# An attention stage on one core: one query tile with all sixteen heads as the unit, scores in four row tiles, and the weighting of values half a batch later

## The reference, cut to what matters

```python
q = proj(query, Wq, bq); k = proj(key, Wk, bk); v = proj(value, Wv, bv)   # query: LayerNorm of the rows
scores = einsum('bhqd,bhkd->bhqk', q, k) * 0.25 + mask * -1e9
attn = softmax(scores, axis=-1)
ctx = einsum('bhqk,bhkd->bhqd', attn, v)        # then back to (b, s, 256)
x = x + ctx @ Wo.T + bo
```

## Time and profile before

| what | value |
|---|---|
| median of 3 runs | 937.86 us |
| the profiled execution, its own time | 935.81 us, of which the span is 934.0 us |
| PE, DVE, ACT, POOL busy over the span | 690.8, 714.8, 386.6, 133.5 us |
| mean granted TensorE clock | 0.888 |
| attention, from the first statistics to the last aggregation | 357.8 to 650.6 us |

### The profile page before, as it was taken

The page is one execution under the profiler, slowest core; times in us unless marked ns, Lnnn a source line. Parts: engine busy times, 40 slices in busy tenths (PEclk is TensorE's granted clock), DMA queues, the critical chain, the costliest instruction groups (busy, mean ns, idle before and its releaser), DMA issues.

```text
span 934.0 us, 13856 instructions
## 1 busy us (share of the span) xinstructions
PE 690.8 (74%) x3693; PEld 477.1 (51%) x3694; DVE 714.8 (77%) x1743; ACT 386.6 (41%) x646; POOL 133.5 (14%) x165
## 2 busy tenths in 40 slices
PE   4599853989988885899999999994033666665674
PEld 2487642656566653577776777773021333343343
DVE  4388885565555556888888888887988899999995
ACT  1343311232232320443433434333145787777773
POOL 4547651212212121000000000000000000000000
PEclk9799986999999995999999999998557788778887
DMA  9586533111121118000000000000000000000001
GB/s 326 159 322 227 186 117 95 47 47 47 52 62 53 42 44 314 3 0 0 0 0 0 0 0 0 0 0 2 1 0 1 1 22 23 11 11 22 22 23 45
DMA packets 31362, 54.33 MB, mean 58 GB/s; under 512 B 4877, under 2 KB 24222, under 8 KB 30176
## 3 DMA queue, kind: packets, MB, share of 16 engines
q1 hardware_dynamic: 25184, 39.81, 12.8%
q0 software_dynamic: 5568, 13.58, 4.2%
q10 hardware_dynamic: 576, 0.55, 0.2%
HBM read 39.90 MB, written 15.89 MB: 60 GB/s over the span
## 4 chain that ended last, share of the span: by engine, by line
DVE 32%; PE 25%; issue 17%; ACT 8%; DMA 7%; SPq 4%; POOL 3%; DVEq 2%; POOLq 1%; ACTq 0%
PE bank L1060 6%; PE bank L1033 3%; PE quad L1019 3%; PE quad L1007 3%; DMA x_after_ffn<-row,niU 2%; DVE hh L1903 2%; DMA row<-rows_by_expert 2%; SPq L408 2%; DVE ctxs L1854 2%; PE bank L1223 2%; POOL x_after_ffn L506 2%; DMA xg<-in_x,idxu 2%; PE bank L1048 2%; SPq L409 1%; DVE ctxs L1842 1%
## 5 line engine op out<-in xcount | busy, mean ns | idle before, releaser
L1223 PE MATMUL bank<-dT,hqT 128*128 128x256 bf16 x256 | 53.3, 379 | 44.7 <-ACT hqT L780 44.7
L953 PE MATMUL bank<-W2s,hidT 128*128 x320 | 76.0, 386 | 12.2 <-ACT hidT L619 12.2
L615 ACT ACTIVATE hid<-hid 128x512 f32<-128x512 f32 x40 | 25.2, 631 | 125.1 <-DVE hid L1517 125.1
L1060 PEld LDWEIGHTS bank<-nVB,nPT 128*128 128x128 f32 x512 | 63.3, 191 | 23.9 <-ACT nPT L677 23.1
L953 PEld LDWEIGHTS bank<-W2s,hidT 128*128 128x128 f32 x320 | 59.3, 190 | 28.3 <-issue 21.7
L936 PE MATMUL quad<-W1s,xts 128*128 x160 | 73.0, 600 | 0.0
L1019 PE MATMUL quad<-nKB,nQT 128*128 128x512 f32 x132 | 71.6, 626 | 1.0 <-ACT nQT L655 0.9
L1060 PE MATMUL bank<-nVB,nPT 128*128 128x34 f32 x512 | 65.5, 273 | 0.0
L506 POOL DMA_INDIRECT x_after_ffn<-row,niU x40 | 39.3, 983 | 168.4 <-DVE row L1526 156.5
L1223 PEld LDWEIGHTS bank<-dT,hqT 128*128 128x128 bf16 x256 | 31.8, 132 | 57.3 <-ACT hqT L780 47.4
L673 ACT ACTIVATE nS<-nS 128x512 f32<-128x512 f32 x64 | 40.8, 637 | 38.3 <-DVE nS L1665 37.0
(11 more groups left out here) (322 smaller groups left out, 1581.7 us busy)
## 6 DMA issues: line engine op xcount, KB each, us to landing
row<-rows_by_expert SPq DMA_DIRECT2D x44, 134.0 KB, 2.1
W1s<-in_ctxO SPq DMA_DIRECT2D x4, 1024.0 KB, 7.9
ctxs<-in_ctxT SPq DMA_DIRECT2D x4, 1024.0 KB, 12.7
W1s<-in_W SPq DMA_DIRECT2D x8, 512.0 KB
W2s<-in_W SPq DMA_DIRECT2D x8, 512.0 KB
X<-x_after_ffn SPq DMA_DIRECT2D x8, 512.0 KB, 7.7
out<-yo SPq DMA_DIRECT2D x16, 256.0 KB, 2.1
b1s<-in_b SPq DMA_DIRECT2D x1, 2048.0 KB
```

The lines of the kernel that those rows point to most:

```text
L953: ins = pe.matmul(bank[6 + u % 2][:, 0:D], hidT[:, u % 2, c, :], W2s[:, bass.ds(ex, 1), c, :].rearrange("p o s -> p (o s)"), start=c == 0, ...
L1060: ins = pe.matmul(bank[7][:, n * 2 * VW:(n + 1) * 2 * VW], nPT[j % 2][:, k, :], nVB[h][:, n, :], start=True, stop=True)
L1223: ins = pe.matmul(bank[(1, 7)[u // 2]][:, (u % 2) * D:(u % 2 + 1) * D], hqT[:, u % 2, c, :], dT[:, c, :], start=c == 0, stop=c == FT - 1)
```

## The change

It touches the narrow branch alone.

- The unit is a query tile with all 16 heads: `nS` is 128x1024, `nM` has 16 maxima, `nPT` is 128x1024.
- `score(b, q)` is 8 matmuls (c = 0, 1 and k = 0 to 3). Each has 32 partitions of `nQT` (two heads) as stationary operand and 128 columns of `nKB`, which is now only 2 heads wide (a new tile `own2` masks it). The four k go to four row tiles of the array and to four PSUM banks.
- Banks 2 to 5 hold both the scores (`scored`, columns 0 to 255 of each) and the transposed probabilities (`turned`, columns 256 to 511). So `score` waits until ScalarE has copied `turned` (n_pTe), and `probs_in` until VectorE has read `scored` (n_add).
- `shift(b, q)` is one add and one reduction of 128x1024 and two subtractions of 128x512. `exps` are two of 128x512, `probs_out` one copy of 128x1024, `probs_in` eight transposes, `weigh` eight matmuls.
- `rows_norm` moves from VectorE to ScalarE, as an activation with the scale rs2 and the bias nm2 = -mean x rs2 (one small instruction in `inverse_rows`).
- The order of the calls changes: `probs_in`, `weigh`, `divide`, `project` and `add_rows` of a query tile stand half a batch later against `score` and `shift`, so the scores of batch b+1 stand in batch b, and a half pass more runs after the loop. Before the loop `shift(0, 0)`, `shift(0, 1)` and `keys_values(1)` stand among `some_stats`. `weight_sizes` stands before the last three `add_rows`.
- Queries go through bank 6 in place of bank 2, and GpSimd copies the context one batch further ahead.

```diff
--- before.py
+++ after.py
...
-        nKB = [sb(f"nKB{h}", [P, DC, HG * KW], F32, en) for h in range(2)]
+        nKB = [sb(f"nKB{h}", [P, DC, 2 * KW], F32, en) for h in range(2)]
+        own2 = sb("own2", [P, 2], F32, en)
...
-        nS = [sb(f"nS{h}", [P, HG, KW], F32, en) for h in range(2)]
-        nM = [sb(f"nM{h}", [P, HG], F32, en) for h in range(2)]
+        nS = [sb(f"nS{h}", [P, NH, KW], F32, en) for h in range(2)]
+        nM = [sb(f"nM{h}", [P, NH], F32, en) for h in range(2)]
...
-        nPT = [sb(f"nPT{h}", [P, HG // 2, P], F32, en) for h in range(2)]
+        nPT = [sb(f"nPT{h}", [P, 4, 2 * P], F32, en) for h in range(2)]
...
+        scored, turned = quad[:, :, 0:2 * P], quad[:, :, 2 * P:4 * P]
...
+                def rows_norm(bt):
+                    act.wait_ge(n_ct, bt)
+                    for q in range(2):
+                        t = bt * 2 + (q + 1)
+                        act.activation(xn3[:, q, :], X2[:, bass.ds(t, 1), :].rearrange("p o d -> p (o d)"), ACT.Identity,
+                                       bias=nm2[:, bass.ds(t, 1)], scale=rs2[:, bass.ds(t, 1)]).then_inc(n_xn, 1)
...
+                def exps(b, q):
+                    for k in range(2):
+                        act.wait_ge(n_sub, b * 4 + (2 * q + k + 1))
+                        half = nS[q][:, HG * k:HG * k + HG, :]
+                        ins = act.activation(half, half, ACT.Exp)
+                    ins.then_inc(n_exp, 1)
+                def probs_out(b, q):
+                    act.wait_ge(n_pT, b * 2 + (q + 1))
+                    act.copy(nPT[q][:], turned).then_inc(n_pTe, 1)
+                def batch(b, h, first=False, last=False, end=False):
+                    if not first:
+                        values_out(b - 1, 0)
+                        probs_out(b - 1, 1)
+                    if not last and not end:
+                        rows_out(b + 1)
+                    if not end:
+                        exps(b, 0)
+                    if not last and not end:
+                        rows_norm(b + 2)
+                        queries_out(b + 1, 1 - h)
+                    if not first:
+                        values_out(b - 1, 1)
+                    if not end:
+                        probs_out(b, 0)
+                        exps(b, 1)
...
+                def score(b, h, q, first=False):
+                    if q == 0:
+                        pe.wait_ge(n_qe, b + 1)
+                        pe.wait_ge(n_kb, b + 1)
+                    if first:
+                        if q:
+                            pe.wait_ge(n_add, 1)
+                    else:
+                        pe.wait_ge(n_pTe, b * 2 + (q - 1))
+                    for c in range(DC):
+                        for k in range(4):
+                            w = slice(32 * k, 32 * k + 32)
+                            ins = pe.matmul(scored[:, k, c * P:(c + 1) * P], nQT[h][w, c, q * P:(q + 1) * P], nKB[h][w, c, :],
+                                            start=True, stop=True)
+                    ins.then_inc(n_S, 1)
+                def probs_in(b, q, last=False):
+                    pe.wait_ge(n_exp, b * 2 + (q + 1))
+                    pe.wait_ge(n_add, b * 2 + (q + 1 if last else q + 2))
+                    for c in range(DC):
+                        for k in range(4):
+                            ins = pe.transpose(turned[:, k, c * P:(c + 1) * P],
+                                               nS[q][:, 4 * k + 2 * c:4 * k + 2 * c + 2, :].rearrange("p h s -> p (h s)"), ident[:])
+                    ins.then_inc(n_pT, 1)
+                def weigh(b, h, q, first=False):
+                    pe.wait_ge(n_pTe, b * 2 + (q + 1))
                     if not first:
...
+                        pe.wait_ge(n_cn, b * 2 + q)
+                    for c in range(DC):
+                        for k in range(4):
+                            n = 4 * c + k
+                            ins = pe.matmul(bank[7][:, n * 2 * VW:(n + 1) * 2 * VW], nPT[q][:, k, c * P:(c + 1) * P], nVB[h][:, n, :],
+                                            start=True, stop=True)
+                    ins.then_inc(n_pv, 1)
...
+                def batch(b, h, first=False, second=False, last=False, end=False):
+                    if not last and not end:
+                        keys_values(b + 1, 1 - h)
+                    if not first:
+                        project_turn(b - 1, 0, first=second)
+                        probs_in(b - 1, 1, last=end)
+                        project(b - 1, 0)
+                    if not last and not end:
+                        rows_in(b + 1)
+                    if not end:
+                        score(b, h, 1, first=first)
+                    if not first:
+                        weigh(b - 1, 1 - h, 1)
+                    if not last and not end:
+                        queries(b + 1)
+                    if not first:
+                        project_turn(b - 1, 1)
+                    if not end:
+                        probs_in(b, 0)
+                    if not first:
+                        project(b - 1, 1)
+                    if not last and not end:
+                        score(b + 1, 1 - h, 0)
+                    if not end:
+                        weigh(b, h, 0, first=first)
...
+                def shift(b, q):
+                    v.wait_ge(n_S, b * 2 + (q + 1))
+                    tt(nS[q][:].rearrange("p (k m) s -> p k m s", k=4), scored.rearrange("p k (m s) -> p k m s", m=4),
+                       maskS[:, q, S - KW:S].unsqueeze(1).unsqueeze(1).broadcast_to([P, 4, 4, KW]), ALU.add).then_inc(n_add, 1)
+                    v.wait_ge(n_add, b * 2 + (q + 1))
+                    red(nM[q][:], nS[q][:], AX.X, ALU.max).then_inc(n_max, 1)
+                    v.wait_ge(n_max, b * 2 + (q + 1))
+                    for k in range(2):
+                        half = nS[q][:, HG * k:HG * k + HG, :]
+                        tt(half, half, bc(nM[q][:, HG * k:HG * k + HG], KW), ALU.subtract).then_inc(n_sub, 1)
...
+                def batch(b, h):
+                    divide(b - 1, 0)
+                    add_rows(b - 1, 0)
+                    new_stats(b - 1, 0)
+                    shift(b, 1)
+                    divide(b - 1, 1)
+                    keys_values(b + 1, 1 - h)
+                    add_rows(b - 1, 1)
+                    new_stats(b - 1, 1)
+                    shift(b + 1, 0)
+                stn.link(red(own2[:], ownh[:].rearrange("p (r t) -> p t r", t=2), AX.X, ALU.add))
+                inverse_rows(0, stn)
+                keys_values(0, 0)
                 some_stats(1, stn)
...
+                some_stats(2, stn)
+                shift(0, 0)
+                some_stats(3, stn)
+                some_stats(4, stn)
+                some_stats(5, stn)
+                shift(0, 1)
+                keys_values(1, 1)
+                for k in range(6, NTILE // 4):
                     some_stats(k, stn)
                 inverse_rows(1, stn)
...
+                shift(1, 0)
+                with v.Fori(0, NB // 2 - 1) as i:
+                    stn.enter(i, 8)
+                    batch(i * 2 + 1, 1)
+                    batch(i * 2 + 2, 0)
+                    stn.leave(NB // 2 - 1)
+                b = NB - 1
+                divide(b - 1, 0)
+                add_rows(b - 1, 0)
+                new_stats(b - 1, 0)
+                shift(b, 1)
+                divide(b - 1, 1)
                 weight_sizes()
...
+                add_rows(b - 1, 1)
+                new_stats(b - 1, 1)
+                for q in range(2):
+                    divide(b, q)
+                    add_rows(b, q)
+                    ins = new_stats(b, q)
+                stn.link(ins)
```

More of the change, by code:

```diff
@@ L1026, in project_turn @@
+                def project_turn(b, q, first=False):
+                    pe.wait_ge(n_cn, b * 2 + (q + 1))
+                    if not first:
+                        pe.wait_ge(n_fin, b * 2 + q)
                     for k in range(DC):
```

222 lines of the change are left out of this document (68 added, 154 removed).

## The result

The changed kernel takes 949.48 us (median of 4 runs, 947.01 to 950.82), the kernel before beside it 937.35: a ratio of 1.013, with an interval of 1.010 to 1.016. It is slower, by 12.1 us where 6.4 were forecast. In the two profiled executions (950.27 and 935.81) all of the difference lies in attention: from the first statistic to the next stage's first reciprocal it takes 358.51 to 669.31 = 310.80 us, before 357.82 to 654.18 = 296.36.

The account below looks back on a forecast made before the run. A chain of waits per half batch bounds the changed loop: terms sum to 8.28 us, taken as 8.17, 29 halves 236.9. With the parts around the loop, attention is +6.4: 935.81 becomes 942.2, median 944 us, range 931 to 963.

Parts of the forecast that it names:

- signs of being wrong: Adds waiting for scores, a batch pace under 15.5 us, or a granted clock in attention below 1 would refute the forecast.
- to the end of the aggregations: Behind the loop, from `weight_sizes` at 640.3 us: reductions, three open query tiles and aggregations, ending at 660.2.
- The chain: Loop: `divide`, `project_turn`, `probs_in`, `project`, `add_rows`, `new_stats` and `shift` wait for one another, 8.17 us a half batch.
- The score: TensorE in the loop: row-tiled score matmuls take 0.8 to 1.0 us, off the chain up to about 1.1.
- rival A: Row tiles do not overlap: a score takes 2.05 us and sets the chain, 8.93 a half, 968 us; chance 11%.
- The doubt about changes of tiling mode: TensorE: a tiling mode change drains the engine; four a batch, shown by no row, lying in idle time here.
- Gaps of 1.4 us at 16.49 a batch did not do it: Argument against half clock: TensorE's gaps in the loop before left the granted clock at 1.00.
- Rival E: TensorE, with a gap in each half, falls to half clock: 2.2 us more a half, over 1000 us; chance 3%.
- with the reductions at the same time this wait is hidden: Behind the last aggregation: the wait for GpSimd before the next reciprocal vanishes, giving back 3.6 us.
- Before the loop: VectorE idles about 4 us for `score(0, 0)`, first exponential at 390, queries at half clock, `shift(1, 0)` at 399.
- rival B: Not slower: hand-overs, transposes, rows and wide operations cost their low ends, 7.75 us a half, 932 us; chance 10%.
- rival D: No chain binds; VectorE's sum, some 14 us, sets the batch pace, about 909 us; chance 4%.

Follow-up runs that it names:

- e1: Changed kernel with `divide` of the other query tile between the reduction and the subtractions of `shift`, not behind them: 912.33 us, ratio 0.976 to the kernel before.
- e3: Changed kernel with score matmuls over all 128 partitions instead of row tiles of 32, keys masked eight heads wide: 973.09 us, ratio 1.039 to the kernel before.
- e2: Changed kernel with `probs_in` ahead of `project_turn` on TensorE and ScalarE's copies in the same order: 946.27 us, ratio 1.013 to the kernel before.
- e9: Changed kernel with extra unread TensorE matmuls (7, 7, 8 and 1) only behind the loop: ratio 1.010 to the kernel before.
- e4: Changed kernel with unread matmuls added in TensorE's waits, in the loop and behind it: 951.29 us, ratio 1.017 to the kernel before.
- e7: e5 with `divide` one step earlier, between the add and the reduction of `shift`: ratio 0.975 to the kernel before.
- e6: Changed kernel with the loops of `score` turned, so both matmuls of one row tile stand together: ratio 1.016 to the kernel before.
- e8: Changed kernel with the loop's normalising of rows back on VectorE, ahead of `add_rows`: ratio 1.014 to the kernel before.
- e5: e1 with the three reductions of `weight_sizes` spread over VectorE's waits behind the loop: ratio 0.978 to the kernel before.
- e10: e7 with `keys_values` between reduction and subtractions and, in the last pass, `probs_in(15, 1)` ahead of `project_turn(15, 0)`: ratio 0.967 to the kernel before.
- e11: e10 with 2, 3, 4 and 1 extra unread matmuls behind the loop: 923.30 us, ratio 0.961 to the kernel before.

## Why the prediction was right, and where it was off

The sign, the mechanism and the range were right: no engine's sum but the chain of a half batch sets the pace, and it is no faster than the pace before. One of the prediction's own signs of being wrong came true all the same, a granted clock below 1 in attention; its steps on the clock and on the last wait failed, and both made the kernel slower than forecast. The terms, against the profiled executions:

| part | predicted | measured | difference |
|---|---|---|---|
| first statistic to add of `shift(1, 0)` | 41.2 | 38.65 | -2.5 |
| 29 half batches | 236.9 | 241.76 | +4.9 |
| that add to `weight_sizes` | 4.4 | 4.34 | -0.1 |
| to the end of the aggregations | 19.9 | 23.73 | +3.8 |
| to the reciprocal | 0.4 | 2.32 | +1.9 |
| attention against before | +6.4 | +14.4 | +8.0 |

- **The chain**: 8.17 forecast, 8.17 measured in nearly every half without a dip (adds at 498.32, 506.50, 514.66). The second decimal is luck: the terms of the prediction add up to 8.28, and 8.17 was picked between that and the low ends. Against its terms the shift took 3.79 and not 3.69, and `divide`, TensorE's steps and the rows 0.09, 0.08 and 0.03 less than taken. The wide add is 1.208 us (1.204), the reduction 1.22 (1.23). VectorE waits 1.24 or 2.27 ahead of `add_rows`, TensorE's loads 1.6 ahead of `project_turn`, as forecast; 63.9 us of such waits on VectorE over all. That it is this chain is shown by e1, which shortens it at one place and is 36 us faster in attention.
- **The score**: 0.8 to 1.0 taken, 0.73 measured, off the chain. The nearest row, the column tiles, was the right guide, and e3 shows the other end of the bound (2.02) and its price, 24 us as rival A had it. The doubt about changes of tiling mode (the Trainium skill, page TensorEngine Tiling (Array Packing), section Key Properties) is small here: in e2 the first row-tile load waits for nothing and starts 0.33 or 0.17 us behind the load before it, in e3, where a full load stands in its place, 0.03. That agrees with the page, and it lies off the chain.
- **The clock** is the step that failed. "Gaps of 1.4 us at 16.49 a batch did not do it" took the idle time of the weight loads (1.37 in the earlier trace rows); the matmuls beside them stood still for 0.54, and no longer than that anywhere in the loop before:

```profile
479.41 0.66 PE L1048 MATMUL quad<-ident,nS 128*128 128x128 f32 x4 [0.54 <-ACT nS L673]
```

  In the changed kernel they stand still for 1.2 in each half. Rival E was priced in full form only, half clock for the whole loop. What came were one longer stretch at half clock in the first half batch and three of 3.4 us at 466.5, 483.6 and 565.5. The first, and then one of the three in the matmuls of the key and value projections (2.13 us instead of 1.14 for the latter):

```profile
398.50:405.00 6.50, 6.50 (x27) 5.93 (x28) 3.02 (x5) 0.37 (x1) 0.40 (x1) 0.50 0.01 3
...
466.16 1.64 PE L1027 MATMUL bank<-nCB,WkS 128*128 128x64 f32 x8
467.59 2.13 PE L1030 MATMUL bank<-WvS,nCB 128*128 128x272 f32 x4
```

  Of the +4.9 the first half batch (10.52, half clock from 398.3 to 405.0) has 2.4, the last (9.57, with half clock from 633.8) 1.4, and the three in between (8.39, 8.62 and 8.55) 1.1 together. Behind the loop it is half clock for the most part, +3.8, of which e9 gives back 3.0. The Trainium skill, page TensorE: Matmul & The Clock Gate, section A second HAM failure mode: psum-queue depth-cycling, tells of a kernel whose clock moves up and down because TensorE idles a little between groups of matmuls. Up and down it moves here too, but no run shows the idle time to be the reason. e4, which filled the waits, has no dip, but e3 has none either, with waits of 1.0; and e7 fell to half at 528.9 though its matmuls had covered 28.0 of the 28.9 us before:

```profile
500.00:528.90 28.90, 27.99 (x243) 24.57 (x242) 25.19 (x47) 14.30 (x26) 1.58 (x2) 1.00 0.00 0
529.00:532.40 3.40, 3.40 (x13) 2.83 (x13) 2.42 (x3) 0.37 (x1) 0.40 (x1) 0.51 0.00 0
```

- **The wait behind the aggregations**: the step "with the reductions at the same time this wait is hidden" credited GpSimd with all of 3.57. They are two waits that end 0.9 to 1.25 us apart, and the list names only the later. VectorE's own lay right below: 2.3 to 2.7 us in the changed kernel and all twelve experiments. ScalarE's square root, for which the reciprocal also waits, is not the reason: it ends at 667.35, 2.0 before the reciprocal.

```profile
667.02 0.33 ACT L746 ACTIVATE sd<-mv,epsc 128x37 f32<-128x37 f32 x1 [1.32 <-DVE mv L1613]
```

  In the chain above, 2.07 of VectorE's wait is "issue" ahead of an instruction behind a branch, and the DMA view of 665.5 to 670 has packets of the instruction queues (packets, MB, share):

```profile
q8 instruction: 1, 0.02, 1.8%
q14 instruction: 2, 0.02, 1.4%
```

  The Trainium skill, page Runtime: NRT & Kernel Launch, section Instruction fetch mechanics, says that a taken branch out of the loaded pages waits for a fetch. Fetches in this stretch would agree with that, but the view doesn't say for which engine they are, and no run took the branch away.
- **Before the loop** the forecast was 2.5 too long, which hid a part of the miss behind it. The first exponential (389.74) and the cold queries (3.78 at 389.90) came as said, but from there to the add of `shift(1, 0)` it took 7.4 us and not 9 (397.16, forecast 399); the stage itself began 0.7 later.
- **Small slips that move no chance**: the low ends of rival B add up to 7.81, not 7.75. VectorE's sum was put at 15 us a batch before and 14 in rival D; the earlier trace rows give 14.1 before, and 37.05 in 50 at 16.34 a batch are 12.1 after.

The profiles differ in where the clock dips (the halves' mean is 8.34, 8.26, 8.34 and 8.26 in four kernels with the same chain), and the first half batch alone takes 8.2 to 10.5 in them. So 2 to 3 us of any attention time here belong to the one execution, and a difference of that size between two totals shows nothing by itself.

## What to carry to other kernels

Before merging small units into a large one, look at what stands behind it in the same engine's queue: here two subtractions that nobody was waiting for stood ahead of a division for which a whole chain waited, and moving the division ahead of them was worth 36 us in a stage of 311. A wait that is put down to one releaser may have a second right behind it; subtract only the distance between them. And price the clock of an engine for short dips, for the first pass and for the end of a loop, not only for the loop as a whole; compare gaps of matmuls with gaps of matmuls.

## What the runs showed of the hardware

- Loads into four row tiles overlap even for 32-bit data: 16 loads of 32x128 in 0.54 us (0.56 tile by tile), against 16 of 128x128 in 1.86. Going over to row tiles straight from full loads cost 0.14 to 0.3 us (e2 against e3).
- With 43.8 us of matmuls in 50 one kernel (e2) held the full clock through the loop, while the changed kernel with 42.0 to 44.3 fell to half (1.2 of 2.4 GHz) for 3.4 us at a time. In e2 the gap of a half is split in two (matmuls idle 0.32 and 0.62 us, in the next half 0.66 and 0.46), in the changed kernel it is one of 1.2. That is not the reason by itself: e3 held the full clock with a gap of 1.0, and e7 fell without one.
- All eleven dips inside the loops (changed kernel, e6, e7, e8, e9, the first and last half batch left aside) began in the key projection, while TensorE was at work: behind the weighting, 16 records of 34 columns, come 8 of 64. Where one kernel has several, they lie about 82 us, five batches, apart, but for one pair at 17. e4, with 256-column matmuls between the two steps, had none; but e1, e2, e3, e5, e10 and e11 have the same sequence and had none either, so the reason stays open.
- VectorE stood still for 2.07 to 2.42 us behind a branch at the end of a stage, in the traces of the changed kernel and of all twelve experiments.
